# Local attention: the masks of both scorings taken off TensorE, onto VectorE (first scoring) and GpSimd with staircase rows (second scoring)

## The reference, cut to what matters

```python
def local_attention(q, k, v):                 # window of queries: 128
    bk, bv = (look_around(bk), look_around(bv))   # keys: the window before, and its own
    sim = jnp.einsum('bhwid,bhwjd->bhwij', bq, bk)
    mask = (i < j) | (i > j + WINDOW) | (j == -1)
    sim = jnp.where(mask, -jnp.finfo(sim.dtype).max, sim)
    attn = jax.nn.softmax(sim, axis=-1)
    return jnp.einsum('bhwij,bhwjd->bhwid', attn, bv)
```

## Time and profile before

| | |
|---|---|
| runs | 3534.86 us median of 3 (3532.56 to 3538.28) |
| profiled execution | 3537.87 us, span 3536.2 us |
| mean granted TensorE clock | 0.954 of full |
| busy, share of the span | PE 89%, DVE 67%, ACT 49%, POOL 22% |
| local attention, both layers | about 606 us each: 1731.5 to 2337 and 2614.8 to 3221 of the span |

### The profile page before, as it was taken

The page is one execution under the profiler, slowest core; times in us unless marked ns, Lnnn a source line. Parts: engine busy times, 40 slices in busy tenths (PEclk is TensorE's granted clock), DMA queues, the critical chain, the costliest instruction groups (busy, mean ns, idle before and its releaser), DMA issues. The chain is left out here.

```text
span 3536.2 us, 76024 instructions
## 1 busy us (share of the span) xinstructions
PE 3162.5 (89%) x31852; PEld 1928.2 (55%) x31852; DVE 2373.5 (67%) x3284; ACT 1722.9 (49%) x3173; POOL 785.7 (22%) x757
## 2 busy tenths in 40 slices
PE   7799999999999999998689999959968999995995
PEld 6433333344443433343467777647856777764784
DVE  7699998987899988772356555535535655553554
ACT  4267777887678888886033333222213333322221
POOL 7400000000110000001043333312224333331221
PEclk9699999999999999997899999979989999997998
DMA  7420001000210000000300000000010000000004
GB/s 242 130 61 17 9 9 45 9 14 13 59 39 9 13 13 5 5 8 23 127 24 14 20 20 14 8 32 0 0 34 24 14 20 20 14 8 32 0 0 143
DMA packets 62014, 113.62 MB, mean 32 GB/s; under 512 B 9608, under 2 KB 25480, under 8 KB 61192
## 3 DMA queue, kind: packets, MB, share of 16 engines
q1 hardware_dynamic: 57608, 102.84, 9.5%
q10 hardware_dynamic: 4096, 6.30, 0.7%
HBM read 74.77 MB, written 33.55 MB: 31 GB/s over the span
## 5 line engine op out<-in xcount | busy, mean ns | idle before, releaser
L649 DVE TENSOR_REDUCE mp<-ps_m 128x2 f32<-128x1024 f32 (+3 forms) x1152 | 1275.7, 1135 | 186.2 <-PE ps_m L700 132.9
L627 ACT ACTIVATE probs<-ps_s 128x512 f32<-128x512 f32 (+3 forms) x2304 | 1162.6, 561 | 372.8 <-PE ps_s L724 342.2
L740 PE MATMUL ps_o<-probs,vall 128*32 128x256 f32 (+3 forms) x9216 | 708.4, 379 | 15.7 <-POOL probs L604 9.1
L724 PE MATMUL ps_s<-qst,kst 64*128 64x512 f32 (+3 forms) x2304 | 593.0, 484 | 4.5 <-ACT probs L627 3.1
L700 PE MATMUL ps_m<-kst,qst 64*128 64x512 f32 (+3 forms) x2304 | 479.1, 399 | 33.4 <-DVE mp L649 15.8
L724 PEld LDWEIGHTS ps_s<-qst,kst 64*128 64x128 f32 x2304 | 240.7, 186 | 457.2 <-ACT probs L627 399.3
L740 PEld LDWEIGHTS ps_o<-probs,vall 128*32 128x32 f32 x9216 | 185.5, 109 | 339.8 <-issue 175.3
L700 PEld LDWEIGHTS ps_m<-kst,qst 64*128 64x128 f32 x2304 | 231.8, 191 | 78.0 <-DVE mp L649 58.7
L989 POOL TENSOR_TENSOR a_rot<-a_t 128x512 f32<-128x512 f32 x128 | 163.0, 1273 | 448.6 <-DVE a_t L1344 448.6
L1514 ACT ACTIVATE m_gl<-m_bank_u,m_b 128x512 f32<-128x512 f32 x96 | 66.3, 691 | 344.4 <-PE m_bank_u L77 344.4
L1035 ACT ACTIVATE a_sq<-a_BP 128x512 f32<-128x512 f32 x128 | 76.6, 599 | 292.8 <-PE a_BP L77 292.8
(11 more groups left out here) (182 smaller groups left out, 5271.3 us busy)
## 6 DMA issues: line engine op xcount, KB each, us to landing
a_tab<-in_rope SPq DMA_DIRECT2D x32, 512.0 KB
q_parts<-pparts SPq DMA_DIRECT2D x32, 256.0 KB, 3.9
k_parts<-pparts SPq DMA_DIRECT2D x32, 256.0 KB, 3.9
qst<-q_parts SPq DMA_DIRECT2D x64, 128.0 KB, 2.6
o_raw<-o_sb SPq DMA_DIRECT2D x32, 256.0 KB, 2.1
X<-in_x SPq DMA_DIRECT2D x8, 512.0 KB, 6.1
kst<-k_parts SPq DMA_DIRECT2D x32, 128.0 KB, 3.7
qst<-q_parts SPq DMA_DIRECT2D x64, 64.0 KB, 2.6
```

Of the source, the lines that this page charges most:

```text
L627: act.activation(probs[:, s % PR, h, off:C], sslots[n % SR][:, off:C], ACT.Exp, scale=float(D) ** -0.5).then_inc(exp_done, 1)
L649: dve.tensor_reduce(mp[b % 2][:, h:h + 2, cc:cc + 1], slot[:, :, 0:width], AX.X, ALU.max).then_inc(max_read, 1)
L724: pe.matmul(sslots[n % SR][:, off:C], kst[g % 2][rows, hp, i * P:(i + 1) * P], qst[q_slot(b)][rows, hp, off:C], start=True, stop=True).the ...
L740: last = pe.matmul(ps_o[32 * h:32 * h + VW, lo:hi], vall[:, i, (g * GH + h) * DV:(g * GH + h) * DV + VW], probs[:, s % PR, h, lo:hi], star ...
```

## The change

The first scoring no longer starts with mask matmuls. Its first products carry `start=True`, and VectorE adds the mask from a float32 table in SBUF while it takes the maximum: eight `tensor_tensor_reduce` (add, then maximum) of 256 columns, one for each head and half, written back to `SU` in place, with a small memset ahead of them, where two `tensor_reduce` of 1024 columns stood. `max_done` counts eight for each window instead of two.

The second scoring has no mask matmuls either. Sixteen rows beside the two of `-max` in each group of 32 hold -1e30 for the block of eight queries that a query lies in (they are turned along with `-max` from `msp`, which is preset with them), and the weights `rows_own` and `rows_next` are ones where a key's block lies beyond the query's: this masks in steps of eight (a staircase). The piece of -1e30 rows and `-max` comes as one matmul of 128 columns for each own and next window. What is left inside the diagonal blocks GpSimd sets to zero after the exponential, with `affine_select` on `PT` (`trim`), two selects of 4 x 128 columns for each window and half of the heads; `weigh` waits for `trim_done`. The three tables come in one load of 128 x 288 float32, staged in `sq`, and VectorE copies them.

```diff
         id_sb = sb("id", [P, P])
-        idb_sb = sb("idb", [P, P], BF16)
-        mask = sb("mask", [P, 2 * N2], BF16)
+        mask = sb("mask", [P, N2])
+        idle = sb("idle", [P, 1])
...
-        row1 = sb("row1", [P, P], F32R)
+        rows_own, rows_next = (sb(f"rows{i}", [P, P], F32R) for i in "on")
...
+        table = sq[:, 0, :, :].rearrange("p a b -> p (a b)")[:, 0:2 * P + HQ]
...
         @block.gpsimd
...
+            def trim(kb, b):
+                if win(kb):
+                    pool.wait_ge(exp_done, 2 * kb + b + 1)
+                    part = PT[:, kb % PR, 2 * b:2 * b + 2, :].rearrange("p i (q c) -> p (i q) c", q=2)
+                    own = pool.affine_select(part[:, :, 0:P], part[:, :, 0:P], pattern=[[0, 4], [1, P]], compare_op=ALU.is_ge,
+                                             fill=0.0, base=0, channel_multiplier=-1)
+                    own.then_inc(trim_done, 1)
+                    if kb + 1 < NT:
+                        pool.affine_select(part[:, :, P:N2], part[:, :, P:N2], pattern=[[0, 4], [-1, P]], compare_op=ALU.is_ge,
+                                           fill=0.0, base=0, channel_multiplier=1).then_inc(trim_done, 1)
+
             for k in range(NI + 4):
                 low_part(k - 4, 1)
+                trim(2 * k - 6, 1)
+                trim(2 * k - 5, 0)
                 if live(k):
                     for g in range(4):
+                        if g == 2:
+                            trim(2 * k - 5, 1)
...
+                else:
+                    trim(2 * k - 5, 1)
+                trim(2 * k - 4, 0)
                 low_part(k - 3, 0)
...
-            def mask_unit():
-                for i in range(4):
-                    pe.matmul(SU[:, i, :], idb_sb[:, :], mask[:, :], start=True, stop=False, skip_group_check=True)
 
             def score_max(w):
                 if w >= 1:
-                    pe.wait_ge(max_done, 2 * w)
+                    pe.wait_ge(max_done, 8 * w)
...
-                mask_unit()
...
-                                                 QK[rows, 4 * q + 2 + d, at:at + n], start=False, stop=(d == 1),
+                                                 QK[rows, 4 * q + 2 + d, at:at + n], start=(q == 0 and d == 0 and s == 0), stop=(d == 1),
...
             def score_turned(kb):
...
-                mask_unit()
...
-                for q in range(2):
-                    for at, off, n in runs:
+                for part, rows_by in enumerate((rows_own, rows_next)[0:2 if kb + 1 < NT else 1]):
+                    at = ((kb + part) % RW) * P
+                    for q in range(2):
                         for i in range(4):
                             rows = slice(32 * i, 32 * i + 32)
-                            pe.matmul(SU[:, i, q * N2 + off:q * N2 + off + n], row1[rows, :], negm[rows, q, at:at + n],
-                                      start=False, stop=False, tile_position=(32 * i, 0), skip_group_check=True)
+                            pe.matmul(SU[:, i, q * N2 + part * P:q * N2 + part * P + P], rows_by[rows, :], negm[rows, q, at:at + P],
+                                      start=(part == 0 and q == 0), stop=False, tile_position=(32 * i, 0), skip_group_check=True)
...
                 if q == 0:
                     pe.wait_ge(exp_done, 2 * (2 * p + 2))
+                    pe.wait_ge(trim_done, min(4 * (2 * p + 2), 4 * NT - 2))
...
+            dve.tensor_copy(rows_own[:, :], table[:, 0:P]).then_inc(set_done, 1)
+            dve.tensor_copy(rows_next[:, :], table[:, P:2 * P]).then_inc(set_done, 1)
+            dve.tensor_copy(msp[:, :, :, :, :].rearrange("p a b c d -> p (a b c) d"),
+                            table[:, 2 * P:2 * P + HQ].rearrange("p (o d) -> p o d", o=1).broadcast_to([P, 16, HQ])
+                            ).then_inc(set_done, 1)
...
             def row_max(w):
...
                 lo = 0 if w else P
-                for b in range(2):
-                    dve.tensor_reduce(mx[:, w % 2, 2 * b:2 * b + 2, :],
-                                      SU[:, 2 * b:2 * b + 2, :].rearrange("p i (q c) -> p i q c", q=2)[:, :, :, lo:N2],
-                                      AX.X, ALU.max).then_inc(max_done, 1)
-                dve.wait_ge(max_done, 2 * (w + 1))
+                dve.memset(idle[:, :], 0.0)
+                for i in range(4):
+                    for q in range(2):
+                        dve.tensor_tensor_reduce(SU[:, i, q * N2 + lo:(q + 1) * N2], SU[:, i, q * N2 + lo:(q + 1) * N2], mask[:, lo:N2],
+                                                 1.0, -3.0e38, ALU.add, ALU.max, mx[:, w % 2, i, q:q + 1]).then_inc(max_done, 1)
+                dve.wait_ge(max_done, 8 * (w + 1))
```

More of the change, by code:

```diff
@@ L868, in _, with local_attention_layer @@
                                       bo_sb[:, :].rearrange("p (o e) -> p o e", o=1).broadcast_to([P, 2, E]), ALU.add).then_inc(y_out, 1)
-def local_attention_layer(nc, layer, X, w_qkv, w_o, rope, scale_cols, ident, identb, window_mask):
+def local_attention_layer(nc, layer, X, w_qkv, w_o, rope, scale_cols, ident, window_mask, window_rows):
     with ExitStack() as ctx:
@@ L922, in local_attention_layer @@
         B7 = psum("B7", [P, 512])
+        trim_done = sem("trim")
         const_in, wq_in, wo_in = sem("const_in"), sem("wq_in"), sem("wo_in")
@@ L953, in _ @@
             sp.dma_start(stage[:, 0:EC * 3 * INNER], w_qkv).then_inc(wq_in, 16)
-            for dst, src in ((id_sb[:, :], ident), (idb_sb[:, :], identb), (mask[:, :], window_mask), (sc_sb[:, :], scale_cols)):
+            for dst, src in ((id_sb[:, :], ident), (mask[:, :], window_mask), (sc_sb[:, :], scale_cols), (table, window_rows)):
                 sp.dma_start(dst, src).then_inc(const_in, 16)
@@ L966, in _ @@
             pool.memset(half[:, :], -0.5).then_inc(half_set, 1)
-            pool.memset(msp[:, :, :, :, :].rearrange("p a b c d -> p (a b c d)").bitcast(F32), 0.0).then_inc(set_done, 1)
             pool.memset(ones[:, :], 1.0).then_inc(set_done, 1)
@@ L1005, in _ @@
             act.wait_ge(wl_done, 2)
-            act.wait_ge(set_done, 10)
+            act.wait_ge(set_done, 8)
             def weights(kb):
@@ L1091, in _ @@
             pe.wait_ge(wl_done, 2)
-            pe.wait_ge(set_done, 10)
-            def mask_unit():
-                for i in range(4):
-                    pe.matmul(SU[:, i, :], idb_sb[:, :], mask[:, :], start=True, stop=False, skip_group_check=True)
+            pe.wait_ge(set_done, 8)
             def score_max(w):
                 if w >= 1:
-                    pe.wait_ge(max_done, 2 * w)
+                    pe.wait_ge(max_done, 8 * w)
                 if w >= 3:
                     pe.wait_ge(exp_done, 2 * (w - 2))
-                mask_unit()
                 a = (w % RW) * P
@@ L1107, in score_max @@
                     for d in range(2):
-                        for at, off, n in (spans(w - 1, 2) if w else [(0, P, P)]):
+                        for s, (at, off, n) in enumerate(spans(w - 1, 2) if w else [(0, P, P)]):
                             for i in range(4):
@@ L1116, in score_turned @@
             def score_turned(kb):
-                pe.wait_ge(max_done, 2 * min(kb + 3, NT))
+                pe.wait_ge(max_done, 8 * min(kb + 3, NT))
                 if kb >= 1:
@@ L1294, in _ @@
             dve.memset(blocks[:, :], 0.0).then_inc(clear_done, 1)
-            dve.memset(row1[:, :].bitcast(F32), 0.0).then_inc(clear_done, 1)
-            dve.wait_ge(clear_done, 2)
+            dve.wait_ge(clear_done, 1)
             for i in range(4):
                 dve.memset(blocks[32 * i:32 * i + 32, i:i + 1], 1.0).then_inc(set_done, 1)
-                dve.memset(row1[32 * i:32 * i + 2, :].bitcast(F32), 1.0).then_inc(set_done, 1)
             dve.wait_ge(wh_done, 1)
@@ L1308, in _ @@
             dve.wait_ge(nsc_done, 1)
-            dve.wait_ge(set_done, 10)
+            dve.wait_ge(set_done, 8)
             def row_max(w):
@@ L1715, in build @@
         local_attention_layer(nc, layer, X, t["w_lqkv" + n], t["w_lo" + n], t["rope"], t["rope_scale" + n], t["ident"],
-                              t["identb"].bitcast(BF16), t["window_mask"].bitcast(BF16))
+                              t["window_mask"], t["window_rows"])
         mlp_layer(nc, layer, X, t["w_1" + n], t["w_2" + n], t["b_1" + n], t["ln" + n], t["b_2" + n], t["ident"],
@@ L1781, in lay_out @@
     both = np.concatenate([np.where(c < r, MASKED, 0.0), np.where(c > r, MASKED, 0.0)], 1)
-    arr["window_mask"] = bf16_bits(np.tile(both, (1, 2)))
+    arr["window_mask"] = np.ascontiguousarray(both.astype(np.float32))
+    block = np.arange(P) // 8
+    rows_own, rows_next = np.zeros((32, P), np.float32), np.zeros((32, P), np.float32)
+    rows_own[0:2], rows_next[0:2] = 1.0, 1.0
+    rows_own[2:18] = block[None, :] > np.arange(16)[:, None]
+    rows_next[2:18] = block[None, :] < np.arange(16)[:, None]
+    hot = np.zeros((P, 32), np.float32)
+    hot[:, 2:18] = np.where(block[:, None] == np.arange(16)[None, :], MASKED, 0.0)
```

(1 more changed line is left out.)

## The result

The kernel after runs in 3489.34 us (median of 4, 3484.4 to 3505.07) against 3533.71 us (median of 4, 3531.43 to 3538.28) for the kernel before: ratio 0.9876, 95% interval 0.985 to 0.9903, 44 us faster. The forecast was 3506, 29 us faster than the 3534.86 that it started from.

A forecast was written before the change was run, and what follows sets the result against it. TensorE was taken to bound the kernel (busy 89%), with thin cover. -23 us in 24 full periods and -6 outside gave -29, so 3506 us from 3534.86; forecast range 3485 to 3524 (chance 0.47), whole range 3474 to 3576.

The forecast's parts named there:

- TensorE's saving: Four mask units a period gone, 3.88 us; each turned scoring 0.16 longer; net -3.56 us a period if TensorE alone counted.
- R: Length of VectorE's whole row maximum, eight steps forecast at 0.46 us each: taken as 3.80 us, bounds 2.9 and 5.07.
- period: Steady stretch between ends of `weigh(k-3, 0)` in local attention: 34.45 us before, 33.50 forecast, 24 in all.
- first half: From the end of `weigh(k-3, 0)` to the output projection: 12.89 us before, forecast 13.49, held by VectorE's chain.
- Serial row maximum: Rival, chance 0.16: in both row maxima nothing overlaps, step 0.63 us, R = 5.07, total 3575 us.
- even trade: Rival, chance 0.12: R between 4.1 and 4.4, so TensorE waits for what it saves; total 3535 us.
- tight overlap: Rival, chance 0.16: the row maximum steps like plain reductions, 0.33 us; total 3474 us.
- 9.69 + R: Forecast length in us of the first half: the row maximum plus 9.69 for the rest of VectorE's and ScalarE's chain.
- The second half: From the output projection to the period's end: 21.56 us before, forecast 19.78 plus a 0.23 wait for the maximum.
- GpSimd at nothing: Eight selects a period, 0.41 to 0.82 us each, fall in GpSimd's idle queue time and were costed at nothing.
- The clock: Rival, chance 0.06: TensorE's longer waits lower its granted clock in each period, +41 us on the forecast, total 3547 us.
- Outside the periods: Parts of the two local attention layers before and behind the full periods: forecast -3 us a layer, -6 in all.

The follow-up runs named there:

- e5: Kernel after with five small memsets, each waiting for the one before, ahead of the row maximum of odd windows (first half): 3528.5 us, ratio 0.9971 to the kernel before.
- e7: Kernel after with two plain reductions over unmasked scores, the maximum scaled by 0.125, and no GpSimd selects: 3471.3 us, ratio 0.9813 to the kernel before.
- e1: Kernel before with only the first scoring's part of the change; the second scoring's mask stays on TensorE, no selects: 3510.59 us, ratio 0.9928.
- e3: Kernel after without GpSimd's selects and without the wait for them: 3486.65 us, ratio 0.986 to the kernel before.
- e4: Kernel after with the row maximum as two plain reductions over unmasked scores, scaled by 0.125, selects kept: 3467.67 us, ratio 0.9812 to the kernel before.
- the four moves together: Kernel after with only written orders on ScalarE and TensorE changed, short operations such as V's copy earlier: 3447.41 us, ratio 0.9743 to the kernel before.

## Why the prediction was right, and where it was off

*TensorE's saving* came as forecast: mask units gone, turned scorings longer by 0.16 us or a little more (L1142 to L1294 is 2.38 us, where L1128 to L1279 took 2.16).

*R* was the mis-sized term: 3.80 forecast, 3.19 measured. By the forecast's own sign the prediction would be wrong with a step outside 0.39 to 0.50 us; the step is 0.38, just outside, and R just under the 3.2 to 4.1 that it gave to its forecast. The time lies within the 3485 to 3524 that went with it. The step had been put together as 0.39 us, the spacing of a two-input operation from PSUM, plus 0.07 for the readout. The first number was right (0.38). The readout adds nothing that can be seen: it starts with the next operation, and the step that includes it is no longer than the 0.39 us of the two-input operation without one. The Trainium skill, page "VectorE: DVE Perf Modes", section "Two Vector instructions with no wait between them", counts two instructions, and the trace agrees (512 reads beside 512 operations); but the second is no addition to the path. The forecast noted that without the readout its sum would come out some 20 us lower. By its own formula it is 17: R = 7 x 0.39 + 0.48 + 0.10 = 3.31, a period of 32.78, 3489 us. That this is the measured time is in part luck, for the misses below cancel: 0.29 us in the first half against 0.32 in the second, and a slow tail beside them. (The upper edge of its range for R = 4.1, 3524, is 3521 by the same formula.) *Serial row maximum* and *even trade* fall with a step of 0.38. So does the step of 0.33 of *tight overlap*: that rival's time was nearer than the forecast's in the end (15 us against 17), but not by its mechanism, and the 342 ns worked out beside it are short of the measured 0.38 us too.

*The first half.* The chain 9.69 + R held in its form: e5 and e7 move it one for one, e1 shows that TensorE's work doesn't count in it. Its constant measured 9.40. In numbers it was forecast at 13.49 and is 12.59 (this period): 0.61 of the difference is R; 0.14 is the memset and the start, since the first step begins 0.07 us before `on` has ended and the memset runs inside it; 0.12 is `negm`, which I had put in at its length of 0.38 where V starts 0.26 us behind it; 0.03 is the rest of the way to `on`. So "the first half gets longer" was wrong in sign: it is 0.30 us shorter than the same stretch before (12.89). By the forecast's own formula it gets longer only from R = 3.20 on (12.89 - 9.69), and R came out at 3.19.

*The second half* was forecast at 20.01, of which 0.23 was a wait that R = 3.80 would have brought. There is none (R is under the 3.57 from which it would start), so 19.78 was due. Measured in this period: 20.10, 0.32 more, all of it in distances on TensorE: 0.19 from the projection to `score_max(2k-2)` (5.82 us against 5.63), 0.07 from there to the turned scoring, 0.06 in the turned scoring. Part of the 0.19 is that a scoring behind a projection now starts 0.21 us after it, where the mask group started at 0.12: the mask unit had taken that changeover on itself.

*The period* is 32.80 by the mean against 33.50 forecast; with R = 3.19 put in, the same formula gives 12.88 + 19.78 = 32.66. TensorE's wait for `mx` in the first half was forecast at about 1.3 us and is 0.41; that for `on`, 0.46, was not named. The period of before on which the forecast stood was a short one, 34.45 where the mean of 11 is 34.59.

*GpSimd at nothing* held (e3): 0.63 us a select, inside the bounds of 0.41 and 0.82; no engine waits for one, and `rot` still has 5.91 us of idle time ahead of it where it had 8.39. But the cover was looked for in GpSimd's queue only. What e4 and e7 show, that it can be paid in VectorE's time, was not among the costs.

*The clock* rival fell in the periods: 2.92 us of idle time a period left the granted clock at 1.00.

*Outside the periods* the forecast was 6 us beside 24 full periods; beside the same 24, 3.4 were won. The start of the layers, up to T0 of k = 4, gave 3.8 (2.0 and 1.8). Behind the periods nothing was won: step k = 16 takes 28.64 us, in the kernel before 28.49, although TensorE is busy 21.40 us in it instead of 23.69. The granted clock of that step is 0.88 where it was 0.94, and the forecast had no term for it. In e1 the same step takes 31.7 us at 0.84. These are one profile each; no experiment separates what the clock costs there from what the waits cost.

## What to carry to other kernels

When work moves from the engine that bounds to one that is nearly idle by its share, write down the chain of the receiving engine through the stage, part by part, and add up starts, not lengths: most errors here were lengths put where an overlapped start was meant. For the operation that the trace lacked, the spacing of its nearest kin alone (0.39 us) came within 0.01 us of the measured step; the second instruction that came with it, priced on top, did not lie on the path. When the remaining waits are each for a short operation queued behind a long one, moving the short ones ahead can be worth as much as the change itself (42 us here for the four moves together, against 44).

## What the runs showed of the hardware

- An accumulator read (145 ns by itself) starts in the same instant as the next operation of VectorE: `tensor_tensor_reduce` of 256 columns steps by 0.38 us with its read, where `scalar_tensor_tensor` of 256 columns steps by 0.39 without one.
- A VectorE operation of 8 columns between SBUF tensors took 0.64 us instead of 0.17 when it met GpSimd's subtraction of 512 columns, and ended with it. In e4_plain_max 26 of its 64 instances met that subtraction and took 0.60 to 1.27 us, and 26 met a select and took 0.27 to 0.28; each of these 52 ended 27 to 34 ns after GpSimd's instruction. `tensor_tensor_reduce` on PSUM ran beside that same subtraction (in the kernel after, 1948.34 to 1949.63) with its spacing unchanged. The Trainium skill, page "SBUF — State Buffer", section "SBUF: two separate sides", says that the two engines share a pair of ports, which whoever starts first holds for the whole instruction, and that some VectorE operations need it. That fits these 52 instances and e7, but not all of the trace: four times in e4_plain_max the same operation began while GpSimd's power `rn` ran, which reads SBUF too, took its 0.17 us and ended 1.2 us before it. One of the four, VectorE's row and then GpSimd's:

```profile
1785.64 0.17 DVE L1343 TENSOR_SCALAR a_msp<-a_mx 128x8 fp32r<-128x8 f32 x1
```

```profile
1781.56 5.45 POOL L1011 TENSOR_TENSOR a_rn<-a_ssc,a_half 128x32 f32<-128x32 f32 x1
```

That the ports are the cause, rather than something else that the two share, was not tested by itself.

- A select of 512 elements a partition on GpSimd takes 0.63 us, one of 256 took 0.41; an estimate from these two is 0.86 ns an element and some 0.19 us fixed.
